# Last stage of a four-layer model: the plan of work written in half steps, two-half products on 128x1024 tiles, ReLU on ScalarE and the gate after the down projection

## The reference, cut to what matters

```python
# L3 attention: x is normed; xs = silu(conv(x @ in_w.T) + conv_b); 256 channels, 16 states
delta = softplus(xs @ wd1.T @ wd2.T + wd2_b)
A, Bm, Cm = -exp(A_log), xs @ wb.T, xs @ wc.T
def step(h, inp):
    d_l, b_l, c_l, x_l = inp
    h = exp(d_l[:, :, None] * A) * h + (d_l * x_l)[:, :, None] * b_l[:, None, :]
    return (h, einsum('ben,bn->be', h, c_l))
y = (scan(step) + xs * W_D) * silu(skip)
x = layernorm(x + y @ out_w.T)
# L3 ffn: gate = softmax probabilities kept by a top-p rule (0.8), zero elsewhere
h = relu(einsum('bth,ehf->betf', x, W1) + b1)        # 8 experts, 512 hidden
y = einsum('betf,efh->beth', h, W2) + b2
x = layernorm(x + einsum('bte,beth->bth', gate, y))
```

## Time and profile before

| what | value |
|---|---|
| median of 3 runs (lowest to highest) | 2513.61 us (2507.25 to 2520.78) |
| time of the profiled execution | 2509.93 us |
| its span, first to last instruction | 2508.1 us |
| PEld, DVE, ACT, POOL busy share of the span | 62%, 70%, 43%, 36% |
| scans of the merged stage, first and last start | 1558.6 and 2395.6 us |
| mean granted PE clock | 0.933 of full speed |

### The profile page before, as it was taken

How to read it: one execution, slowest core, us unless ns; L and a number is a source line. 1 busy time by engine, 2 the same in 40 slices (tenths; PEclk the granted TensorE clock), 3 DMA queues, 4 the chain that set the end, 5 groups by cost and what they waited for, 6 DMA issues and landing times. The chain is left out here.

```text
span 2508.1 us, 32976 instructions
## 1 busy us (share of the span) xinstructions
PE 2197.8 (88%) x11383; PEld 1565.0 (62%) x11383; DVE 1759.1 (70%) x3455; ACT 1077.0 (43%) x2455; POOL 905.0 (36%) x751
## 2 busy tenths in 40 slices
PE   7888778799799999999994975787998989898998
PEld 3565556688699898989883862333454544454455
DVE  6667555677566767676764873877878787878954
ACT  6231322598544554455442543553434343442310
POOL 4000000211222233323332552876555564555610
PEclk9798899999899999999995996888999999999999
DMA  9400000000000000000000343323243334333411
GB/s 363 142 1 1 1 1 1 1 1 1 19 1 1 4 8 11 11 1 11 11 11 27 90 157 99 102 90 96 80 115 85 106 90 109 89 100 97 114 36 34
DMA packets 77150, 145.25 MB, mean 58 GB/s; under 512 B 9432, under 2 KB 31080, under 8 KB 75944
## 3 DMA queue, kind: packets, MB, share of 16 engines
q1 hardware_dynamic: 72600, 133.67, 18.0%
q0 software_dynamic: 4384, 9.46, 1.2%
HBM read 130.91 MB, written 31.65 MB: 65 GB/s over the span
## 5 line engine op out<-in xcount | busy, mean ns | idle before, releaser
L209 PE MATMUL ps<-TMP,W 128*128 128x512 f32 (+5 forms) x1232 | 613.4, 616 | 36.9 <-ACT TMP L224 9.1
L209 PE MATMUL ps<-TMP 128*128 128x65 f32 (+5 forms) x4370 | 523.5, 287 | 7.1 <-DVE W L229 4.4
L209 PEld LDWEIGHTS ps<-TMP 128*128 128x128 f32 (+3 forms) x4370 | 475.3, 191 | 63.2 <-issue 28.6
L233 POOL TENSOR_TENSOR TMP<-TMP 128x512 f32<-128x512 f32 (+1 forms) x176 | 231.2, 1318 | 609.2 <-ACT TMP L224 437.9
L224 ACT ACTIVATE TMP<-ps,W 128x256 f32<-128x256 f32 (+2 forms) x528 | 283.1, 582 | 285.6 <-DVE TMP L229 162.1
L233 POOL TENSOR_TENSOR TMP<-TMP,W 128x512 f32<-128x512 f32 x256 | 333.9, 1328 | 196.0 <-DMA W<-rows 180.0
L209 PEld LDWEIGHTS ps<-TMP,W 128*128 128x128 f32 (+3 forms) x1232 | 223.9, 192 | 259.7 <-issue 195.3
L209 PE MATMUL ps<-TMPr,Wr 128*128 128x512 f32 x768 | 318.7, 523 | 18.6 <-DVE TMP L232 18.2
L209 PE MATMUL ps<-TMPr 128*128 128x512 f32 (+4 forms) x1032 | 264.0, 401 | 34.0 <-DVE TMPr L229 22.6
L232 DVE SCALAR_TENSOR_TENSOR TMP<-ps,SM,XK 128x512 f32<-128x512 f32 x256 | 189.0, 739 | 100.5 <-PE ps L209 99.9
L209 PEld LDWEIGHTS ps<-TMPr,Wr 128*128 128x128 f32 x768 | 145.4, 192 | 164.4 <-issue 107.2
(11 more groups left out here) (239 smaller groups left out, 3014.4 us busy)
## 6 DMA issues: line engine op xcount, KB each, us to landing
W<-rows SPq DMA_DIRECT2D x224, 256.0 KB, 4.7
sorted<-pad SPq DMA_DIRECT2D x8, 2304.0 KB
XK<-gates SPq DMA_DIRECT2D x64, 256.0 KB, 3.5
TMP<-rows SPq DMA_DIRECT2D x32, 256.0 KB, 4.6
TMP<-sorted SPq DMA_DIRECT2D x72, 72.0 KB, 2.0
W<-wp SPq DMA_DIRECT2D x1, 4124.0 KB, 15.5
XK<-results SPq DMA_DIRECT2D x16, 256.0 KB, 3.9
W<-wp SPq DMA_DIRECT2D x1, 3072.0 KB, 26.4
```

Of the source, the lines that this page charges most:

```text
L209: return nc.tensor.matmul(out, lhsT, rhs, start=start, stop=stop, **k)
L233: gtt = lambda o, a, b, op: nc.gpsimd.tensor_tensor(o, a, b, op)
```

## The change

Each point names the steps concerned.

- The plan is written in half steps q (two a state). A side step that needs another engine's result stands a half step or more behind it; "conv" is split into "conv" and "conv2", two products each; the parts of the gates' chain stand at q+16, 18, 19, 20, 22, "row" at q+24, "row_out" at q+25, the store ("table") at q+27, the fetches at q+28, where they had filled the two states before the "fetch".
- `Ub`, `Hb`, `Cb` are 128x1024 tiles (3, 2, 3 in place of 6, 4, 6 halves). "head" and "read" are one instruction a state, with the row broadcast over the halves. Scans stay 512 wide.
- Loads of the B row are issued four states ahead ("b_row"), of the C row three ("c_row"), the store of a chunk's rows ("rows_out") in the chunk before; all of them had been at "head", two states ahead.
- "hid" is an ACT ReLU with bias b1 into `hg`. "down" accumulates over the 4 units of an expert. "gated" on DVE computes (po + b2) * gate once an expert, into `yg`; the next expert's first "down" waits for it. "join" on POOL adds `yg` to x once an expert.
- The steps "bias", "bias_turn", "bias_rows", "bias_negated" and "bias_in" are gone.

```diff
-        Bb, Cr, Ub, Hb, Cb = (more(n) for n in (4, 4, 6, 4, 6))
+        Bb, Cr = more(4), more(4)
+        whole = lambda n: [ar(1024) for _ in range(n)]
+        Ub, Hb, Cb = whole(3), whole(2), whole(3)
+        two = lambda row: row.unsqueeze(1).to_broadcast([128, 2, 512])
...
-        first_unit = 16 + 13
+        first_unit = 32 + 26
...
+        for q in range(-8, first_unit + NU + 4):
+            (g, s), u = divmod(q, 2), q - first_unit
+            if s == 0 and 0 <= g + 4 < GN:
+                plan.append(("b_row", g + 4))
+            if s and 0 <= g + 3 < GN:
+                plan.append(("c_row", g + 3))
+            if s == 0 and 0 <= g + 2 < GN:
                 plan.append(("head", g + 2))
...
+            plan += ahead(u + 1) + hidden(u)
+            if 0 <= g < GN:
+                plan.append(("scan", (g, s)))
+            plan += gated(u - 2) + joined(u - 3)
+            if 0 <= g - 2 < GN:
+                plan.append(("tail", (g - 2, s)))
+                if (g - 2) % 16 == 15:
+                    plan.append(("output", ((g - 2) // 16, s)))
+            plan += beside.pop(q, [])
+            if 0 <= g + 1 < GN:
+                plan.append(("decay", (g + 1, s)))
+            if s and 0 <= g < GN:
+                plan.append(("read", g))
+            plan += down(u - 1)
...
                 elif step == "down":
                     i, x, c = a
-                    e.wait_ge(*hid_dve.at(a))
-                    mm(po, tile(W2, 4 * x + c), hg[nth[a] % 4], False, x == 7 and c == 3).then_inc(*dn_pe(a))
+                    e.wait_ge(*hid_act.at(a))
+                    if c == 0 and i + x:
+                        e.wait_ge(*gy_dve.at(experts[8 * i + x - 1]))
+                    mm(po, tile(W2, 4 * x + c), hg[nth[a] % 4], c == 0, c == 3).then_inc(*dn_pe(a))
...
+                elif step == "hid":
...
+                    e.wait_ge(*up_pe.at(a))
+                    if n >= 4:
+                        e.wait_ge(*dn_pe.at(units[n - 4]))
+                    act(hg[n % 4], ups[n % 2], ACT.Relu, bias=w("B1")[:, unit:unit + 1]).then_inc(*hid_act(a))
...
-                    stt(hg[n % 4], ups[n % 2], nB1[:, unit:unit + 1], gd[q % 3], ALU.max, ALU.mult).then_inc(*hid_dve(a))
...
+                    tt(g3(Cb[a % 3], 2), two(Cr[a % 4]), g3(Hb[a % 2], 2), ALU.mult).then_inc(*hc_dve(a))
...
+                    stt(yg[q % 2], po, w("B2")[:, x:x + 1], gd[q % 3], ALU.add, ALU.mult).then_inc(*gy_dve(a))
...
-                        gtt(Ub[q % 6], ch(dx, x), Bb[a % 4], ALU.mult).then_inc(*u_pool((a, x)))
+                    gtt(g3(Ub[a % 3], 2), g3(dx, 2), two(Bb[a % 4]), ALU.mult).then_inc(*u_pool(a))
...
+                    gtt(ch(XT, i), ch(XT, i), yg[(8 * i + x) % 2], ALU.add).then_inc(*join_pool(a))
```

More of the change, by code:

```diff
@@ L2349, in skip_gate @@
[L2349 to L2355, removed]
-            n = norm(7, i)
[L2357 to L2369, removed]
@@ new lines, in skip_gate, with hand_over @@
+        def skip_gate(i, q):
+            put(q + 18, ("open", (i, 0)))
+            put(q + 19, ("open_out", (i, 0)))
+            put(q + 20, ("gate", (i, 0)))
+            put(q + 21, ("open", (i, 1)))
+            put(q + 22, ("open_out", (i, 1)))
+            put(q + 23, ("gate", (i, 1)))
+        def hand_over(i, q):
+            n = norm(7, i)
+            put(q + 5, ("out", i))
+            put(q + 6, ("result", i))
+            put(q + 7, n[0])
+            put(q + 8, n[1])
+            put(q + 9, n[2])
+            put(q + 10, n[3])
+            put(q + 12, n[4])
+            put(q + 13, n[5])
+            put(q + 14, n[6])
+            put(q + 15, n[7], ("split", i))
+            put(q + 16, ("shift", i))
+            put(q + 18, ("probs", i))
+            put(q + 19, ("route", (i, 0)))
+            put(q + 20, ("route", (i, 1)))
+            put(q + 22, ("route", (i, 2)))
+            put(q + 24, ("row", i))
+            put(q + 25, ("row_out", i))
+            put(q + 27, ("table", i))
+            put(q + 28, *[("fetch", 8 * i + k) for k in range(3)])
@@ L2382, in scan_moe_stage @@
[L2382 to L2385, removed]
+        plan += [("softplus", (0, 0)), ("softplus", (0, 1)), ("exp", 0), ("log", 0), ("dx", 0), ("rows_out", 0)]
+        put(-2, norm(6, 1)[3])
+        put(-1, *norm(6, 1)[4:])
+        for i in range(NCH + 1):
+            q = 32 * i
+            if i >= 1:
+                hand_over(i - 1, q)
+            if i < NCH:
+                skip_gate(i, q)
             if i + 1 < NCH:
-                prepare(i + 1, 16 * i if i else 2)
-                skip_gate(i + 1, 16 * i + 12 if i else 14)
+                prepare(i + 1, q)
@@ L2389, in scan_moe_stage @@
             if i + 2 < NCH:
[L2390 to L2399, removed]
+                norm_ahead(i + 2, q)
@@ L2400, in scan_moe_stage, with hidden, down, gated @@
+            if i >= 2:
+                last_norm(i - 2, q)
         for x in range(8):
-            put(17 + x, 1, ("weights", x))
+            put(35 + 2 * x, ("weights", x))
         def ahead(j):
-            if j >= NU:
+            if not 0 <= j < NU:
+                return []
+            return [("up", units[j])]
+        def hidden(j):
+            return [("hid", units[j])] if 0 <= j < NU else []
+        def down(j):
+            return [("down", units[j])] if 0 <= j < NU else []
+        def gated(j):
+            if not 0 <= j < NU or units[j][2] < 3:
@@ L2405, in ahead, with joined @@
                 return []
             i, x, c = units[j]
[L2407 to L2414, removed]
+            return [("gated", (i, x))]
+        def joined(j):
+            if not 0 <= j < NU or units[j][2] < 3:
                 return []
             i, x, c = units[j]
-            out = [("bias_in", i)] if x == c == 0 else []
-            return out + [("down", units[j])] + ([("join", i)] if x == 7 and c == 3 else [])
@@ L2420, in scan_moe_stage @@
[L2420 to L2424, removed]
-                plan.append(("head", g + 2))
[L2426 to L2445, removed]
@@ L2446, in scan_moe_stage @@
-        for j in range(2 * (GN + 16 - first_unit), NU):
-            plan += behind(j) + ahead(j + 1) + down(j - 1)
-        plan += down(NU - 1) + norm(8, NCH - 1)
+            return [("join", (i, x))] + ([("fetch", 8 * i + x + 3)] if x < 5 else [])
+        for q in range(-8, first_unit + NU + 4):
[5 more added lines that the diff above has]
+            if s == 0 and 0 <= g + 2 < GN:
+                plan.append(("head", g + 2))
+            plan += ahead(u + 1) + hidden(u)
[12 more added lines that the diff above has]
+            plan += down(u - 1)
@@ L2449, in scan_moe_stage @@
+        plan += norm(8, NCH - 1)
         assert not beside, beside
@@ L2464, in scan_moe_stage @@
         raw_act = Sig(sem("s7_b_rows"), I)
-        a_act, u_pool, h_dve, y_pe = (Sig(sem("s7_" + n), GE) for n in ("decay", "input", "state", "y_sum"))
-        hc_dve, hc_pool = (Sig(sem("s7_read_" + n), [(g, e) for g, e in GE if by_pool(g) == p]) for n, p in (("dve", False), ("pool", True)))
-        read = lambda g, x: (hc_pool if by_pool(g) else hc_dve).at((g, x))
+        a_act, h_dve, y_pe = (Sig(sem("s7_" + n), GE) for n in ("decay", "state", "y_sum"))
+        u_pool = Sig(sem("s7_input"), G)
+        hc_dve, hc_pool = (Sig(sem("s7_read_" + n), [g for g in G if by_pool(g) == p]) for n, p in (("dve", False), ("pool", True)))
+        read = lambda g: (hc_pool if by_pool(g) else hc_dve).at(g)
         c_act = Sig(sem("s7_carried"), [(g, e) for g, e in GE if g // 16 % 2 == 0])
@@ L2485, in scan_moe_stage @@
         w_high, w_low = Sig(sem("moe_weights_high"), range(8)), Sig(sem("moe_weights_low"), range(8))
-        nb_dve, bi_pe, bi_dve, bi_turn, bi_act = (Sig(sem("moe_bias_" + n), (0,)) for n in ("negated", "pe", "sum", "turned", "rows"))
-        up_pe, hid_dve, dn_pe = (Sig(sem("moe_" + n), units) for n in ("up", "hidden", "down"))
-        ct_pe, join_dve = Sig(sem("moe_bias_in"), I), Sig(sem("moe_joined"), I)
+        up_pe, hid_act, dn_pe = (Sig(sem("moe_" + n), units) for n in ("up", "hidden", "down"))
+        experts = [(i, x) for i in I for x in range(8)]
+        gy_dve, join_pool = Sig(sem("moe_gated"), experts), Sig(sem("moe_joined"), experts)
         stored_at = lambda i: (s_gst[i % 2], 16 * (i // 2 + 1))
@@ L2494, in scan_moe_stage @@
         for s, a in plan:
[L2495 removed]
+            if s in ("open", "conv", "rank", "bc", "delta", "centre", "back", "back2", "logits", "out", "row"):
                 takers.append((s, a))
         first_bank = {("conv", (0, 0)): 7, ("conv", (0, 1)): 5, ("rank", 0): 6, ("bc", 0): 4, ("delta", (0, 0)): 7, ("delta", (0, 1)): 5,
[L2498 removed]
+                      }
         for i in range(2):
@@ L2507, in scan_moe_stage @@
         let_go = {"open": gt_dve, "conv": ev_act, "rank": rk_act, "bc": raw_act, "delta": ab_act, "back": n_xa, "back2": n_xk,
```

(10 more changed lines are left out.)

202 lines of the change are left out of this document (92 added, 110 removed).

## The result

The changed kernel takes 2481.68 us (median of 4, 2479.16 to 2482.66) against 2512.93 us for the kernel before on the same chip: a ratio of 0.987, 95% interval 0.984 to 0.990. The forecast was 2477 us in a range of 2442 to 2516. Ratios are of fast executions alone: three slow ones, 2679.56 us of the kernel before, 2866.54 of gate_exp_apart and 4344.63 of pool_narrow, are left out.

The account below looks back on a forecast made before the run. PE was taken as the bound, with DVE holding it up some 15 us a chunk. 2509.9 - 50 - 6.8 + 24 + 4 - 6 + 1.4 = 2476.5, stated as 2477 us, range 2442 to 2516.

Parts of the forecast that it names:

- the clock of the second regime: Sign to look for: PE's mean clock at 0.98 or more in the stretch where every half state carries a unit.
- Spacing the side steps: PE's waits once a chunk for "hid" and "row", and the slow clock after, go in six chunks: -50 us.
- the 8.3 us: PE's loss a chunk: 2.02 us waiting for "hid", 4.32 at the "row" turn, 1.94 at the lower clock.
- Wide products: POOL gains or loses nothing; DVE waits longer at the shared port but stays under PE's chunk: 0 on the path.
- mean wait of 0.96 us a step: Wait of a randomly arriving DVE two-input step for a POOL product, with POOL busy 74 of 104 us a chunk.
- as long as PE covers it: Condition for costing DVE's longer waits at 0: DVE's chunk of 81 us stays under PE's 104.
- Rival C: DVE's two-input steps queue behind POOL's products at the shared port, making DVE the bound: 2552 us, chance 0.13.
- "hid" to ACT: Moves 23.6 us a chunk off DVE, adds 21.9 to ACT; covered as long as PE is the bound.
- The new stalls: PE waits for "gated" and for ACT freeing bank 7: 0 to 12 us a chunk, taken as 4, +24 over six.
- the last way to be wrong: PE waits for "hid" on ACT, because ACT stands at a decay whose scan is late.
- The first stretch: States without units: spacing removes some DVE idle time, longer locks return part; -19 to +15 us, taken as -6.
- the 6.8 us for the bias rows: Dropping "bias_in", one fp32 product of 0.85 us in PE's beat, 8 times: -6.8 us.

Follow-up runs that it names:

- gate_exp_apart: Changed kernel with ACT's gate exponential one half state later than the logarithm; ratio 0.983 to the kernel before, 906.4 us from first scan to end.
- pool_narrow: Changed kernel with POOL's products in two 128x512 instructions each, DVE's left wide; ratio 0.978 to the kernel before, 887.9 us from first scan to end.
- before_spaced: Kernel before with only the row turn and its copy moved later, fetches behind them; ratio 0.996 to the kernel before, 932.2 us from first scan to end.
- hybrid_apart: Changed kernel, gate exponential half a state later, POOL's products wide for states 0 to 28, then narrow, DVE's wide; ratio 0.979, 891.6 us from first scan to end.
- relu_dve: Changed kernel with the "hid" ReLU on DVE in place of ACT; ratio 0.999 to the kernel before, 787.5 us from first to last unit.
- late_rows: Changed kernel with row store and B and C row loads back at the input product, two states ahead; ratio 0.990, 919.4 us from first scan to end.
- narrow: Changed kernel with DVE's and POOL's products in two 128x512 instructions each; ratio 0.985 to the kernel before, 903.4 us from first scan to end.
- open_later: Changed kernel with POOL's products halved and the second skip product half a state later on PE; ratio 0.975, 884.1 us from first scan to end.

## Why the prediction was right, and where not

The time (2482 for 2477) and the sign were as forecast. The chunk was not quite: between its first scans it takes 110.5 us (1831.8 to 2163.4 in three) for 112.9 before (1853.7 to 2192.5), where 107 to 109 were named. Two other signs missed as well: the clock of the second regime is 0.97 where 0.98 was named, and the wide reads take 1.29 and 1.80 us where 1.9 to 2.4 were. PE stays the bound, the "row" wait and its slow clock went, early loads did nothing, and the end cost 1.8 us for 1.4. From first scan to end -30.5 us stand against -33.4 of the sum. But terms of the sum were off in opposite directions.

*Spacing the side steps, -50.* The step that says the 8.3 us go failed in size. before_spaced shows the row wait closed for 20 us among the units, 17 in the stage: of 8.3 us a chunk the 2.0 for "hid" stayed, and 3 came back as waits for "hid" and at the bank, since DVE had not caught up. I had named nothing as the lower bound and taken the upper one. In the changed kernel, where "hid" has left DVE as well, the old waits are all gone (25.0 us for "row" and 17.3 for "hid", 1714 to 2396), and 37.6 us of others stand in their place (1700 to 2354). So the shortfall can be booked here or under the new stalls; the runs do not part the two.

*Wide products, 0 on the path.* This was wrong. pool_narrow shows that POOL's width costs the changed kernel 31 us among the units. My mean wait of 0.96 us a step was about right for the 32-wide steps (1.04 us whole, 0.19 for the unhindered) and four times too long for the wide reads, which take 1.46 us on average (with the one other wide product of a chunk) for 1.22 free, where I had 2.18. DVE's sum (78 us busy for the 81 forecast) came out near with both. What failed is "as long as PE covers it": the lock hits the two gate steps that ACT's exponential waits for, and ACT's list has the ReLUs behind it. That chain is not all of the 31 us: with wide products left in place, gate_exp_apart takes it apart for 13.7, and hybrid_apart gains another 15 by POOL's width. Part of this is waits for "gated", six of 1.8 to 2.0 us in the changed kernel and none over 1 us in pool_narrow; how the rest comes about is not shown. A mean under the bound does not tell what a chain of three engines makes of it. Rival C named the lock, but as DVE's throughput; what counted was its place in the chains that PE waits for.

*"hid" to ACT, cover.* It was costed at zero and is worth 21 us among the units with the wide products in place (relu_dve), two thirds of what POOL's width costs there.

*The new stalls, +24.* They were too small and their place was partly wrong: 16.8 us for DVE steps, 16.2 for ReLUs and 4.6 for ACT's copies, and the slow clock behind them. The waits for a ReLU, which stands behind table loads, were in the prediction only as the last way to be wrong, and for another reason: ACT stood at the gates' exponential, not at a decay. Moving that one 0.2 us activation is worth 13.7 us with what follows from it. Waits for "gated" are there, 2.0 us at most.

*The first stretch, -6.* It was -16.6. DVE was busy 132 of 139 us there. It is not the loads (late_rows), not ReLU (relu_dve) and not POOL's width (pool_narrow). With DVE's products narrow it is 6 us longer (narrow), so some 6 of the 16.6 us are the wide reads. The rest may be the order in half states or the once-only bias products that left this stretch; no run parts them, and none took the 6.8 us for the bias rows alone.

So the time was hit with the help of terms that cancelled, which is luck in part: among the units 15.6 us came for the 28.8 of the sum, in the first stretch 16.6 for 6.

## What to carry to other kernels

A stall taken out of a bound engine is worth its length only if the engine that caused it has caught up by the next wait; price the next wait, not the gap (before_spaced, 17 to 20 us for 38; open_later, 3.8 for 2.7 a chunk). When two engines share a port, the length of one's instruction is a latency for the small steps of the other. Here it paid to merge products on DVE, which serves the chain that PE waits for, and to keep POOL's short (pool_narrow, 887.9 us for 920.1 wide and 903.4 narrow on both). Look at what stands in one list between a late producer and a frequent short step: half a state of distance there was worth nearly half as much as the whole change (13.7 of 30.5 us).

## What the runs showed of the hardware

A 32-wide DVE product with both inputs in SBUF took 0.58 us on average beside POOL products of 1.3 us, 1.04 beside those of 2.6, and 0.70 when these were halved again. The unhindered ones took 0.19 us in all three; the longest took 1.10, 2.29 and 1.20 us. The scans, with one input in PSUM, took 1.19 to 1.29 us in every run.

In the changed kernel each of PE's five waits of 3.0 to 4.0 us for a ReLU is met by a stretch of half the granted clock (1.2 in place of 2.4 GHz) that begins between 1.0 us ahead of its end and 1.3 us behind it; so are two of the six waits of some 1.9 us. In pool_narrow, where five waits of 2.4 to 2.7 us are the longest, only those that end at 1827.3 and 2144.8 have one. In open_later no wait among the units is over 1.9 us, and the granted clock is 1.00 from the first to the last of them.
